# Attention operands stored in DRAM in the layout in which they are loaded, and a filler product in every step that has no other one

## What is computed

```python
q, k, v = split(x @ qkv_w.T)                          # 16 heads of 16
raw = einsum('bhid,bhjd->bhij', q, k)
scores = alpha * tanh(raw / beta)
soft = tanh(x @ hex_w.T); hexc = tanh(x @ q6_w.T)     # 6 codes each per token
scores += lam * einsum('bid,bjd->bij', soft, soft) / 2
scores += einsum('bid,hde,bje->bhij', hexc, Mh, hexc) / 6 * s
attn = softmax(where(causal, scores, -inf)); out = attn @ v
```

## Time and profile before

| | |
|---|---|
| median of 3 executions | 2024.34 us (2022.81 to 2042.44) |
| profiled execution, its own time | 2022.98 us |
| its span in the trace | 2021.2 us |
| PE busy | 1811.4 us, 90% |
| DVE, ACT, POOL busy | 1209.0, 1233.8, 512.2 us |
| mean granted TensorE clock | 0.926 of full speed |
| DMA | 280.29 MB, 139 GB/s over the span |

### The profile page before, as it was taken

One profiled execution on the slowest core, in us unless ns is written; L12 is line 12 of the kernel. 1 busy time (PEld: TensorE's weight loads), 2 busy tenths in 40 slices (PEclk: granted clock), 3 DMA queues, 4 the chain that ended last, 5 costly groups with the idle time before them and its releaser, 6 DMA issues. The chain is left out here.

```text
span 2021.2 us, 33603 instructions
## 1 busy us (share of the span) xinstructions
PE 1811.4 (90%) x10688; PEld 1076.5 (53%) x10689; DVE 1209.0 (60%) x2539; ACT 1233.8 (61%) x1292; POOL 512.2 (25%) x535
## 2 busy tenths in 40 slices
PE   2868999999999979999999997689559999999997
PEld 1333333333334333333333334568459999999997
DVE  7446768878778757778777775867313333333332
ACT  1157889989989968999999993234213333333332
POOL 0535331331232333411000001405612222222222
PEclk7768879989989979999999998889779999999999
DMA  4489674564562477754844404631366666666663
GB/s 152 122 215 187 157 149 102 118 121 110 121 126 70 114 186 147 138 124 108 191 76 76 87 6 133 203 122 69 110 204 182 182 180 175 186 181 181 176 183 79
DMA packets 186101, 280.29 MB, mean 139 GB/s; under 512 B 18512, under 2 KB 120784, under 8 KB 183824
## 3 DMA queue, kind: packets, MB, share of 16 engines
q1 hardware_dynamic: 172272, 259.94, 51.1%
q0 software_dynamic: 13440, 17.97, 4.5%
q10 hardware_dynamic: 288, 1.08, 0.2%
HBM read 213.90 MB, written 65.03 MB: 138 GB/s over the span
## 5 line engine op out<-in xcount | busy, mean ns | idle before, releaser
L963 DVE SCALAR_TENSOR_TENSOR probs<-probs,scal,bil_ps 128x512 f32<-128x512 f32 (+1 forms) x1152 | 788.2, 715 | 286.2 <-PE bil_ps L817 233.5
L896 ACT ACTIVATE probs<-probs 128x2048 f32<-128x2048 f32 (+1 forms) x288 | 522.7, 1815 | 101.5 <-DVE probs L963 101.0
L889 ACT ACTIVATE probs<-raw_ps 128x2048 f32<-128x2048 f32 (+1 forms) x288 | 508.9, 1767 | 28.9 <-PE raw_ps L800 28.4
L817 PE MATMUL bil_ps<-u_mv,w_st 50*128 50x512 f32 (+3 forms) x1280 | 470.9, 469 | 38.0 <-DVE probs L963 33.5
L817 PEld LDWEIGHTS bil_ps<-u_mv,w_st 50*128 50x128 f32 x1280 | 196.3, 192 | 528.9 <-DVE probs L963 448.6
L1635 ACT ACTIVATE hid_t<-fc_ps,b 128x128 f32<-128x128 f32 x576 | 156.3, 382 | 403.4 <-PE fc_ps L1602 236.0
L836 PE MATMUL o_ps<-probs,v_sb 128*32 128x512 f32 (+3 forms) x2560 | 314.5, 575 | 19.4 <-POOL probs L714 13.2
L800 PE MATMUL raw_ps<-q_mv,k_st 64*128 64x512 f32 (+3 forms) x1280 | 270.8, 406 | 15.2 <-DMA q_mv<-q_split 9.5
L1602 PE MATMUL fc_ps<-rows_t,w 128*128 128x128 f32 x2304 | 270.5, 276 | 0.0
L1602 PEld LDWEIGHTS fc_ps<-rows_t,w 128*128 128x128 f32 x2304 | 264.6, 193 | 0.1
L1613 PE MATMUL fc_ps<-w,hid_t 128*128 x1152 | 260.5, 379 | 0.0
(11 more groups left out here) (213 smaller groups left out, 1356.9 us busy)
## 6 DMA issues: line engine op xcount, KB each, us to landing
w<-in_w SPq DMA_DIRECT2D x80, 1024.0 KB, 6.0
q_mv<-q_split SPq DMA_DIRECT2D x128, 128.0 KB, 7.6
k_st<-k_split SPq DMA_DIRECT2D x48, 256.0 KB, 8.5
rows<-x_rows SPq DMA_DIRECT2D x72, 130.0 KB, 2.2
v_rows<-rows_sb SPq DMA_DIRECT2D x8, 1024.0 KB, 7.7
o_t<-o_sb SPq DMA_DIRECT2D x32, 256.0 KB, 9.4
k_st<-k_split SPq DMA_DIRECT2D x16, 512.0 KB, 8.6
v_sb<-v_rows SPq DMA_DIRECT2D x8, 1024.0 KB, 13.6
```

The costliest lines, as they stand in the source:

```text
L817: mm = pe.matmul(bil_ps[:, hd % 2, column:column + width], w_st[row:row + BIAS_ROWS, b, kt * P:(kt + 1) * P], u_mv[row:row + BIAS_ROWS, p, ...
L889: act.activation(probs[:, s % NBUF, :, first:BLK], raw_ps[:, :, first:BLK], ACT.Tanh).then_inc(tanh_ready, 1)
L896: act.activation(scores, scores, ACT.Exp).then_inc(exp_ready, 1)
L963: dve.scalar_tensor_tensor(scores, scores, scal[:, ALPHA:ALPHA + 1], bil_ps[:, hd % 2, first:BLK], ALU.mult, ALU.add).then_inc(sum_ready, 1)
```

## The change

DRAM now holds keys and queries in four parts of 16 rows for each head, in the order of the tiles, and one tensor `u_split` holds all 50 bias rows of each head. A Q part is stored with four DMAs instead of two, the soft rows are written once for every head, with a broadcast source, and the lattice and guard rows go to their places in `u_split`. Loads: two DMAs over all 128 partitions for keys and queries, two over 50 partitions for the bias rows, one for the values. In the preparation of block 0 the stores of Q2 and Q3 are issued by ACT, behind its copies of the high halves. Every step without a piece gets a filler, 173 instead of 111; behind part C it has 64 output rows (64 to 127 of the bank, while C's result lies in rows 0 to 11) and waits for nothing.

```diff
-        if half != 0 and s >= last + (3 if o == "C" else 2):
-            FILL_AT[s] = (i, o)
+        assert half != 0
+        FILL_AT[s] = (i, o)
...
-    scratch("q_split", (B * H * 2 * HD, T))
-    scratch("k_split", (B * H * 2 * HD, T))
-    scratch("lat_split", (B * H * 4 * HEX, T))
-    scratch("soft_split", (B * 4 * HEX, T))
+    scratch("q_split", (B * H * 4 * HD, T))
+    scratch("k_split", (B * H * 4 * HD, T))
+    scratch("u_split", (B * H * BIAS_ROWS, T))
     scratch("code_split", (B * 2 * 4 * HEX, T))
-    scratch("guard_split", (B * H * 2, T))
...
-        N_QK, N_W, N_S, N_L, N_G, N_V = 2, 4, 4, 4, 2, 1
-        N_KEYS, N_BIAS, N_CODES = 10, 6, 2
+        N_QK, N_W, N_S, N_L, N_G, N_V = 4, 4, 4, 4, 2, 1
+        N_KEYS, N_BIAS, N_CODES = 2, 2, 2
...
+        def store_heads(eng, i, m):
+            b, c = BLOCKS[i]
+            halves = (qk_hi, qk_lo, qk_hi, qk_lo) if m < 2 else (qk_hi, qk_lo, qk_lo, qk_hi)
+            for part, src in enumerate(halves):
+                eng.dma_start(part_rows("q_split" if m < 2 else "k_split", H, 4, HD,
+                                        slice((m % 2) * 8, (m % 2) * 8 + 8), part, b, c),
+                              src[:, m, :].bitcast(F32)).then_inc(st_qk[m], 16)
...
-                        sp.dma_start(part_rows("soft_split", 1, 4, HEX, slice(0, 1), part, b, c),
-                                     (s_hi, s_lo)[part % 2][HEX:HROWS, :].bitcast(F32)).then_inc(st_s, 16)
+                        src = (s_hi, s_lo)[part % 2][HEX:HROWS, :].bitcast(F32).rearrange("r (o t) -> r o t", o=1)
+                        sp.dma_start(bias_rows(i, (4 + part) * HEX, HEX).rearrange("z h r t -> r (z h) t"),
+                                     src.broadcast_to([HEX, H, BLK])).then_inc(st_s, 16)
...
+                for dst, name, cols in ((k_st[:, p, :, seen], "k_split", seen), (q_mv[:, p, :, :], "q_split", own)):
+                    rows = heads(name, ROWS, i, g, cols).rearrange("(j r) t -> r j t", r=2 * ROWS)
+                    sp.dma_start(dst.bitcast(F32), rows).then_inc(keys_in[p], 16)
...
+                rows = heads("u_split", BIAS_ROWS, i, g, own).rearrange("(j z r) t -> z r j t", z=2, r=BIAS_ROWS)
                 for z in range(2):
-                    row = z * ROWS
-                    load(u_mv[row:row + n, p, :, :], lat[z])
-                    load(u_mv[row + n:row + 2 * n, p, :, :], sf.broadcast_to([n, HG // 2, BLK]))
-                    load(u_mv[row + 2 * n:row + BIAS_ROWS, p, :, :], gd[z])
+                    sp.dma_start(u_mv[z * ROWS:z * ROWS + BIAS_ROWS, p, :, :].bitcast(F32), rows[z]
+                                 ).then_inc(bias_in[p], 16)
...
-            for o in ("Q0", "C", "Q1", "Q2", "L", "Q3"):
+            for o in ("Q0", "Q1", "C", "L"):
                 store(0, o)
...
                 if o == "C":
-                    pe.wait_ge(code_ready, i + 1)
+                    pe.matmul(part_ps[ROWS:P, :], ident[:, ROWS:P], modrow[:, 0:BLK], start=True, stop=True)
                 else:
                     pe.wait_ge(emptied, EMPTIED[i, o])
-                pe.matmul(part_ps[:, :], ident[:, :], modrow[:, 0:BLK], start=True, stop=True)
+                    pe.matmul(part_ps[:, :], ident[:, :], modrow[:, 0:BLK], start=True, stop=True)
...
                     high_half(i, m)
+                if i == 0:
+                    for m in (2, 3):
+                        act.wait_ge(emptied, EMPTIED[i, f"Q{m}"])
+                        store_heads(act, i, m)
```

More of the change, by code:

```diff
@@ L489, in load_rows, with bias_rows @@
                              ).then_inc(x_in[i % 2], 16)
+            def bias_rows(i, first, n):
+                view = dram["u_split"].rearrange("(z h r) t -> z h r t", h=H, r=BIAS_ROWS)
+                b, c = BLOCKS[i]
+                return view[b:b + 1, :, first:first + n, c * BLK:(c + 1) * BLK]
             def store(i, o):
@@ L507, in store @@
                         sp.wait_ge(lo_ready, 4 * (i - EARLY) + m + 1)
[L508 to L511, removed]
+                    store_heads(sp, i, m)
                 elif o == "L":
@@ L514, in store @@
                     for part in range(4):
-                        sp.dma_start(part_rows("lat_split", H, 4, HEX, slice(0, H), part, b, c),
+                        sp.dma_start(bias_rows(i, part * HEX, HEX).rearrange("z h r t -> (z h) r t"),
                                      (l_hi, l_lo)[part % 2][:, :].bitcast(F32)).then_inc(st_l, 16)
@@ L524, in store @@
                     for part, src in enumerate((g_hi, g_lo)):
-                        dst = part_rows("guard_split", H, 2, 1, slice(0, H), part, b, c)
-                        sp.dma_start(dst.rearrange("h r t -> (h r) t"), src[:, :].bitcast(F32)).then_inc(st_g, 16)
+                        dst = bias_rows(i, 8 * HEX + part, 1)
+                        sp.dma_start(dst.rearrange("z h r t -> (z h r) t"), src[:, :].bitcast(F32)).then_inc(st_g, 16)
             def heads(name, n, i, g, cols):
@@ L554, in load_bias @@
                 b, c = BLOCKS[i]
-                p, n = it % 2, 4 * HEX
+                p = it % 2
                 own = slice(c * BLK, (c + 1) * BLK)
```

## The result

The changed kernel takes **2090.49 us** (median of four runs, 2082.53 to 2090.83) against 2025.5 for the one before (four runs). The ratio is 1.0293, 95% interval 1.0232 to 1.0355: slower by about 65 us, where 2003 us was forecast. The profiled execution took 2090.32 us, its span is 2088.6.

What follows compares the result with a forecast made beforehand. Attention steps exceed 3.63 us where PE's clock falls to half, and in stalls. From 2022.98 us: 28 gained by fillers, 4 lost to them, 9 lost to stores, 6 gained at step 156, so 2002; stated 2003, range 1989 to 2018.

Steps and rivals of the forecast that it cites:

- part 3: Stores of doubled Q parts and 16-fold soft rows: 14.9 us more per block, 9 to 10 us lost, bounds 2 and 16.
- The variant of 5 us: Soft store of six rows gets six DMA engines: its 0.74 MB takes 5 us instead of 3.9, one us worse per block.
- part 2: Key, query and bias loads over more partitions: 1.6 times the old rate, bounds 1 and 2; 12 fewer DMAs per iteration.
- From block 2 on they hide: The added stores spread over 100 us and more from block 2 and hide, as loads come one iteration ahead.
- just covered, 0 to 3 us: Block 0: key loads issued at about 95 us land near 100, before the first score product at 102.07; 0 to 3 us.
- Part 1: A filler in every attention step: ten of eleven clock falls prevented, 28 us gained; 4 us lost in remaining half-clock stretches.
- at full clock that costs nothing: The 62 added fillers cost nothing at full clock, since 45 steps of 3.63 us all have one.
- my lower bound of 15: Gain from fillers in every step halves to 15 us if narrow products (C, G, L) hardly hold PE's clock.
- my mark for being wrong: The forecast is wrong if PE's clock still falls between 230 and 680 us.
- The stall at step 156: PE's wait for values: SP reaches their load about 5 us earlier, 6 us gained, bounds 0 and 8.
- Rival (d): Fillers don't hold the clock and lengthen half-clock steps, adding 31 us: 2057 us, chance 0.03.
- my other marks: Among the signs: iteration 2's keys come between 142 and 158 us; the wait at step 156 is below 2 us.

Runs made afterwards that it cites:

- the run with 96 partitions: The changed kernel with its four soft stores per block read from 96 partitions once each, instead of six read 16 times (wrong values): 2022.44 us, ratio 1.0004.
- the soft rows once: The changed kernel with soft rows stored once per block and spread over the heads by the load, six bias loads per iteration: 2023.24 us, ratio 0.9993.

## Why the prediction was wrong

**The step that failed is part 3's "2.84 MB at 191 GB/s are 14.9 us per block".** The rate was read from Q stores, which leave from 128 partitions, and the soft store's 0.79 MB, 3.9 of the 14.9 us, were priced by it. They leave from six neighbouring partitions at 50 and then 25 GB/s and last about 21 us per block, 17 more. The variant of 5 us, by the Trainium skill ("DMA: Bandwidth & Descriptors", "Why a DMA increments its semaphore by 16 and not by 1"), was wrong for the same reason: it asked how many engines take part. The share of 0.33 is near the six of 16 engines that this rule gives, but with 15 of 16 at work the rate didn't rise. The Trainium skill's port rule stood in part 2, on the loads, and I didn't ask it of the stores. Against the run with 96 partitions (span 2021.9), the change (2088.6) has its first exponential 9.2 us later, loses 19.8 us in step 4, 12.6 in steps 12 to 25, 5.8 in 26 to 143, 12.4 in 144 to 169 and 6.8 behind attention: 66.7.

**"From block 2 on they hide" failed with it.** Hiding was judged by time available and not by what stands behind the stores in the queue: values and keys do, in every block. Steps 12 to 25 (block 2) and 144 to 169 (block 6) show it: at step 13 PE waits for values whose load SP issued at 232.50 us, behind four soft stores and four loads, and which landed at 241.64.

```profile
241.73 1.94 PE L834 MATMUL o_ps<-probs,v_sb 128*32 128x512 f32 x8 [9.31 <-issue]
```

**The rest of part 3 was about right.** With the soft store's source repaired, the wait for iteration 2's keys is 18.4 us (15 to 20 forecast), and its step 4 has an excess of 19.7 us against 10.9, 9 us lost (9 forecast). Block 0, put at "just covered, 0 to 3 us", lost 7.3 us with the soft rows once. Eight issues by ScalarE at "0.6 us each" took up to 3.17 us each in the change, as the engines were taken; alone they matter 3 us.

**Part 1 was right in direction and half the size.** The products brought 11.5 us, not 24. Steps 5 to 169 of the profiled executions show both reasons. 35 steps with half clock became 16, with 41.1 us of excess left of 52.9. Of the eleven falls outside stalls six are gone, not ten, and those that stay are long. The steps at full clock became dearer, 6.9 us of excess against 2.5: "at full clock that costs nothing" was read in a stretch whose steps carry no pieces. With 256 columns that cost is gone (2.0 us).

The five falls that the products left (234.6, 289.3, 565.7, 791.0, 849.0 us) show what the reading of the earlier trace rows missed. One stands in a stall that a product doesn't remove: at step 114 GpSimd gets to a mask only when it has split the codes, PE waits for the mask, and the clock falls. All 15 changed kernels have this wait (4.3 us, with GpSimd's own stores 7.3) and a fall beside it.

```profile
568.22 1.08 PE L836 MATMUL o_ps<-probs,v_sb 128*32 128x256 f32 x8 [4.33 <-POOL probs L714]
```

Before the other four, the 4 us up to the fall hold a narrow product on `part_ps`: G's with 16 columns of weights (234.6, 791.0) or L's over 6 rows (289.3, 849.0, here with a filler behind it). "If the narrow products count as little as the first fall suggests" was the condition of my lower bound of 15, and it fits; no run changed these products, so it is not shown. The changed kernel has four falls between 230 and 680 us, my mark for being wrong: 236.6 in the wait of step 13, 294.7 behind G, 349.3 behind L and 625.8 at the mask. Why runs with the same products have between 9 and 20 steps at half clock is open; each count rests on one execution.

**Part 2 was right in size.** The loads run at 290 GB/s, 1.6 times 180. With the soft rows once there are 10 steps at half clock and 27.7 us of excess in them, against 16 and 41.1 with the products alone; that the faster loads take these falls away is likely and wasn't tested. **The stall at step 156** gave 3.6 us (excess of steps 144 to 169 18.5, then 14.9), not 6, once the soft stores were away, and 5.9 lost in the change.

With the soft rows once, the change's other parts cancel (2022.64 us in the profiled execution, 20 over the forecast). By steps against before: 7.3 us lost up to the first exponential and 2.2 in steps 0 to 3 (0 forecast), 9.6 in step 4 (9 forecast), 20.8 gained in steps 5 to 227 where 28 - 4 + 6 = 30 were forecast, 1.3 lost behind attention. So the store explains all of the slowdown but the 7 us behind attention, and not all of the error. Rival (d), the only slower one, had the wrong place: its extra products lengthened nothing like 31 us. Of my other marks, iteration 2's keys came at 190.82 us, past the 158 that I had set, and the wait around step 156 stayed at 3.19 us, not below 2, with a new one of 5.67 before it.

## What to carry to other kernels

Price a store by the partitions from which it leaves, not by its bytes: a broadcast source on six neighbouring partitions was read at 25 to 50 GB/s here, against 191 from 128 partitions and 283 from 96, and it holds up every transfer on its queue and, through the engines, on others. Multiply small rows in the load instead, as the run with the soft rows once did, or let them leave from more partitions. Try a product that is there only to keep the clock at half its length: 256 columns did better than 512 three times, by 2 to 8 us, and not on the clock. And look for stalls first, since such a product doesn't remove a fall that stands in one.

## What was unexpected of the hardware

Cutting a store so that 0.93 of the engines' time was taken in place of 0.33 made it no faster: 44 against 51 GB/s, all transfers together. A packet of 2 KB took 84, 160, 305 or 1080 ns, by where in SBUF the source partitions lay and how many engines read there at once. What I take for a full queue shows in the issuing engine: issues of 3 to 5 us, and 8.56 us for two. A 32 KB store took 23.8 us to land beside 0.79 MB on another queue. And the bytes themselves were nearly free: 0.74 MB more per block from 96 partitions moved the ratio from 0.9993 to 1.0004, inside both intervals.
